# Merged head transfers, values projected with stationary weights and turned by DMA, and the small loads moved to a later step of a fused attention kernel

## What is computed

```python
h = _L0_tok_ref(L0_tok_log_dt, L0_tok_Lambda, x, 1024)
h = jnp.concatenate([h, txt], axis=1)
h = h + _L0_attn_ref(_layernorm(h), wq, wk, wv, wo)
h = h + _L0_ffn_ref(_layernorm(h), ...)
# _L0_attn_ref: 32 heads, 8 key/value heads of 32, causal
q = (x @ wq).reshape(b, s, NH, HD)
k = (x @ wk).reshape(b, s, NKV, HD)
v = (x @ wv).reshape(b, s, NKV, HD)
scores = jnp.einsum('bihd,bjhd->bhij', q, k) * SCALE
attn = jax.nn.softmax(jnp.where(causal, scores, min), axis=-1)
out = jnp.einsum('bhij,bjhd->bihd', attn, v)
```

## Time and profile before

| | |
|---|---|
| median of 3 runs | 2941.69 us (2940.85 to 2944.85) |
| the profiled execution | 2947.19 us |
| its span, first to last instruction | 2945.1 us |
| TensorE busy | 2695.8 us, 92% |
| VectorE, ScalarE, GpSimd busy | 1940.4, 1201.6, 1144.2 us |
| mean granted TensorE clock | 0.969 of 2.4 GHz |
| `attention`, SyncE's first to last transfer | 213 to 1769 us |
| of it step 0 to step 31 on TensorE | from 329.7 us |
| `tail` | from 1797 us to the end |

### The profile page before, as it was taken

The page is one execution under the profiler, slowest core; times in us unless marked ns, Lnnn a source line. Parts: engine busy times, 40 slices in busy tenths (PEclk is TensorE's granted clock), DMA queues, the critical chain, the costliest instruction groups (busy, mean ns, idle before and its releaser), DMA issues. The chain is left out here.

```text
span 2945.1 us, 70977 instructions
## 1 busy us (share of the span) xinstructions
PE 2695.8 (92%) x27456; PEld 1949.7 (66%) x27456; DVE 1940.4 (66%) x5569; ACT 1201.6 (41%) x2506; POOL 1144.2 (39%) x1811
## 2 busy tenths in 40 slices
PE   1948699999999999999999986999999999999999
PEld 1837589989898998989899972444444444444444
DVE  8964488887888888788888774744444444444443
ACT  4342466676766767666666663101010100101010
POOL 2751266565656656566565563101111010101110
PEclk9978899999999999999999995899999999999999
DMA  7754534434343443435344325354554555454543
GB/s 240 190 123 112 87 88 96 98 77 98 82 102 85 93 98 77 99 82 103 81 95 87 66 55 178 79 139 115 136 123 128 131 119 134 119 140 115 136 122 81
DMA packets 564334, 324.72 MB, mean 110 GB/s; under 512 B 501016, under 2 KB 519704, under 8 KB 563520
## 3 DMA queue, kind: packets, MB, share of 16 engines
q1 hardware_dynamic: 541488, 256.35, 39.2%
q10 hardware_dynamic: 22512, 63.84, 6.9%
HBM read 116.49 MB, written 80.61 MB: 67 GB/s over the span
## 5 line engine op out<-in xcount | busy, mean ns | idle before, releaser
L1018 PE MATMUL psJ<-xth,qh 128*128 128x205 f16 x2048 | 520.3, 254 | 52.4 <-DMA xtl<-xfl 46.9
L689 POOL TENSOR_TENSOR pl<-arena,ph 128x410 f16<-128x410 f32 (+1 forms) x512 | 499.5, 995 | 94.7 <-ACT ph L765 94.7
L1020 PE MATMUL psJ<-xth,ql 128*128 128x205 f16 x2048 | 519.0, 253 | 0.0
L1019 PE MATMUL psJ<-xtl,qh 128*128 128x205 f16 x2048 | 518.6, 253 | 0.0
L684 POOL TENSOR_SCALAR_AFFINE_SELECT arena<-arena 128x256 f32<-128x256 f32 (+1 forms) x768 | 331.6, 438 | 475.5 <-ACT arena L758 454.5
L1243 POOL TENSOR_TENSOR arena<-stage,arena 128x1024 f32<-128x1024 f32 x52 | 122.2, 2349 | 938.1 <-DVE stage L1286 938.1
L1257 ACT CAST xh<-arena 128x1024 f16<-128x1024 f32 x52 | 54.3, 1045 | 998.3 <-DVE arena L1295 998.3
L758 ACT ACTIVATE arena<-psT,escale 128x410 f32<-128x410 f32 (+1 forms) x768 | 401.1, 567 | 119.0 <-PE psT L959 59.7
L765 ACT CAST ph<-arena 128x410 f16<-128x410 f32 (+1 forms) x768 | 334.8, 500 | 15.8 <-POOL arena L684 15.5
L1286 DVE SCALAR_TENSOR_TENSOR stage<-ps5O,osc,h_in 128x512 f32<-128x512 f32 x104 | 78.0, 751 | 390.6 <-PE ps5O L1383 390.6
L860 DVE TENSOR_REDUCE mx<-psS 77x2 f32<-77x410 f32 x512 | 295.4, 577 | 39.8 <-PE psS L1007 32.3
(11 more groups left out here) (234 smaller groups left out, 6143.7 us busy)
## 6 DMA issues: line engine op xcount, KB each, us to landing
a_in<-acat SPq DMA_DIRECT2D x52, 512.0 KB, 3.8
h_in<-hcat SPq DMA_DIRECT2D x52, 512.0 KB, 4.6
qst<-qsh SPq DMA_DIRECT2D x512, 51.2 KB, 2.1
out<-stage SPq DMA_DIRECT2D x51, 512.0 KB, 3.1
hcat<-ob SPq DMA_DIRECT2D x64, 256.0 KB, 4.5
xin<-hcat ACTq DMA_DIRECT2D x32, 512.0 KB
acat<-arena ACTq DMA_DIRECT2D x64, 256.0 KB
qst<-qsl SPq DMA_DIRECT2D x256, 51.2 KB, 2.5
```

The costliest lines, as they stand in the source:

```text
L689: pool.tensor_tensor(view(pl, g % 2, k), view(p32, g % 2, k), view(ph, g % 2, k), ALU.subtract).then_inc(lo_pool, 1)
L1018: pe.matmul(ps[:, 0:S], wh[:, k, c], xth[:, par, k, 0:S], start=k == 0, stop=False)
L1019: pe.matmul(ps[:, 0:S], wh[:, k, c], xtl[:, par, k, 0:S], start=False, stop=False)
L1020: m = pe.matmul(ps[:, 0:S], wl[:, k, c], xth[:, par, k, 0:S], start=False, stop=k == KC - 1)
```

## The change

1. The columns of wq and wk are permuted on the host within each group of four heads, so that the partition of a projected row is (dim, head of four) and not (head of four, dim). One DMA then moves what took four: 3 in place of 12 for each half of queries and each unit of keys. `qst` is laid out as (half, head of four, group) instead of by head, and `mx` with it, and every reader indexes it so.
2. The values are projected as keys are, with the weights stationary and 205 columns streamed. Their two parts go to `vst`, in the last chunk of the staging buffer, SyncE turns them with four DMA transposes a step into `vt` (behind the restack of the first half of the queries), and ScalarE copies them from there beside the ones in `vh` and `vl` in slot 2 of the next step (`values`). There are two buffers of `vh` and `vl`.
3. The staging buffer is in use until the last values are turned, so wo and the 14 small loads are issued in step 30 (b == B - 2), behind the head maxima of slot 0, and no longer in step -1.

```diff
@@ attention, buffers
-        qst = [sb(f"qst{i}", [STACK + 2, NH, S], F16) for i in range(2)]
+        qst = [sb(f"qst{i}", [STACK + 2, 2, REP, NKV // 2, S], F16) for i in range(2)]
-        vh = [sb(f"vh{i}", [P, 2, NKV, HD + 1], F16) for i in range(3)]
+        vh = [sb(f"vh{i}", [P, 2, NKV, HD + 1], F16) for i in range(2)]
...
+        vt = sb("vt", [P, 2, 2, KW], F16)
+        vst = [st[0][:, KC - 1, k * D // 2:(k + 1) * D // 2].bitcast(F16).rearrange("p (c x) -> p c x", c=2)[:, :, 0:2 * P]
+               for k in range(2)]
@@ unit_views, free_place
             if kind == "v":
...
+                return ps[:, 0:S], vst[0][:, n, 0:S], vst[1][:, n, 0:S]
...
-                wait(eng, av_done, 8 * b)
+                wait(eng, v_in[n], 32 * (b + 2))
@@ SyncE
                 for k, src in enumerate(parts_):
-                    rows = dst[k * HD:(k + 1) * HD].rearrange("d (c r) i -> d c r i", r=4)
-                    for r in range(4):
-                        sp.dma_start(rows[:, cs, r, :], src[r * HD:(r + 1) * HD, cs, :]).then_inc(arrived, 16)
+                    sp.dma_start(dst[k * HD:(k + 1) * HD], src[:, cs, :]).then_inc(arrived, 16)
...
-                if b == -1:
-                    sp.wait_ge(w_lo, 2 * KC)
+                if b == B - 2:
+                    for q in v_in:
+                        sp.wait_ge(q, 32 * B)
                     for dst, src, arrived in ahead:
                         sp.dma_start(dst, src).then_inc(arrived, 16)
...
-                    restack(Q_PARTS, qst[par], HALVES[0], q_in[0])
+                    restack(Q_PARTS, qst[par][:, 0], HALVES[0], q_in[0])
+                    wait(sp, v_ok, 2 * (b + 2))
+                    if b == -2:
+                        sp.wait_ge(values_ok, 1)
+                    for c in range(2):
+                        for k in range(2):
+                            sp.dma_start_transpose(out=vt[:, k, :, c * P:(c + 1) * P], in_=vst[k][:, c, :]).then_inc(v_in[c], 16)
                 if has["max"]:
                     wait(sp, pj_lo, base + at(rows, "m", 0) + 1)
                     shift_rows(0, nxt)
@@ ScalarE
+            def values(n):
+                for q in v_in:
+                    act.wait_ge(q, 32 * (n + 1))
+                wait(act, av_done, 8 * (n - 1))
+                for k, dst in enumerate((vh, vl)):
+                    v = vt[:, k].rearrange("p t (g d) -> p t g d", d=HD)
+                    act.copy(dst[n % 2][:, :, :, 0:HD], v).then_inc(v_ok, 1)
...
                     if g == 2 and has["last"]:
                         store(b - 1, 1)
+                    if g == 2 and has["max"]:
+                        values(b + 1)
@@ TensorE
-                if kind in "qk":
+                if kind in "qkv":
                     wh, wl = (qh, ql) if kind == "q" else (kh, kl)
                     c = slice(n * P, (n + 1) * P)
+                    if kind == "v":
+                        c = slice(KW + n * P, KW + (n + 1) * P)
...
-                    m = pe.matmul(ps[:, 0:2 * S], K[:, g, 0:P], Q[:, 4 * g + 2 * k:4 * g + 2 * k + 2, :],
+                    m = pe.matmul(ps[:, 0:2 * S], K[:, g, 0:P], Q[:, g // 4, 2 * k:2 * k + 2, g % 4, :],
@@ kernel (host)
+        if name in ("L0_attn_wq", "L0_attn_wk"):
+            a = a.reshape(D, -1, 4, HD).transpose(0, 1, 3, 2).reshape(D, -1)
```

More of the change, by code:

```diff
@@ L554, in free_place @@
             if kind == "q":
-                wait(eng, q_in[n // 4], 16 * 12 * (b + 2))
+                wait(eng, q_in[n // 4], 16 * 3 * (b + 2))
             if kind == "k":
-                wait(eng, k_in[n], 16 * 12 * (b + 2))
+                wait(eng, k_in[n], 16 * 3 * (b + 2))
             if kind == "v":
-                wait(eng, av_done, 8 * b)
+                wait(eng, v_in[n], 32 * (b + 2))
             if kind == "m":
@@ L585, in step @@
                     wait(sp, pj_lo, before(b - 1, nxt) + at(units(prev), "k", 1) + 1)
-                    restack(K_PARTS, kst[nxt], slice(1, 2), k_in[1])
+                    restack(K_PARTS, kst[nxt][:, 4:8], slice(1, 2), k_in[1])
                     wait(sp, pj_lo, before(b - 1, nxt) + at(units(prev), "q", NKV - 1) + 1)
-                    restack(Q_PARTS, qst[nxt], HALVES[1], q_in[1])
+                    restack(Q_PARTS, qst[nxt][:, 1], HALVES[1], q_in[1])
                 if has["att"]:
@@ L615, in shift_rows @@
             def shift_rows(half, to):
-                heads = slice(half * (NH // 2), (half + 1) * (NH // 2))
-                sp.dma_start(qst[to][STACK:STACK + 1, heads, :], mh[:, half, :]).then_inc(m_in[half], 16)
-                sp.dma_start(qst[to][STACK + 1:STACK + 2, heads, :], ml[:, half, :]).then_inc(m_in[half], 16)
+                sp.dma_start(qst[to][STACK:STACK + 1, half], mh[:, half, :]).then_inc(m_in[half], 16)
+                sp.dma_start(qst[to][STACK + 1:STACK + 2, half], ml[:, half, :]).then_inc(m_in[half], 16)
             def turn(t, to, n):
@@ L646, in _ @@
                 chain(pool.memset(kst[i][STACK:STACK + 2], MROW))
-            for i in range(3):
+            for i in range(2):
                 chain(pool.memset(vh[i][:], 0.0))
                 chain(pool.memset(vl[i][:], 0.0))
-            for i in range(3):
+            for i in range(2):
                 m = pool.memset(vh[i][:, :, :, HD:HD + 1], 1.0)
-                if i < 2:
+                if i < 1:
                     chain(m)
@@ L674, in step @@
                         pool.memset(p32[:, :, 2, :], 0.0).then_inc(late_ok, 1)
+                        for t in vst:
+                            m = pool.memset(t[:, :, S:2 * P], 0.0)
+                        m.then_inc(values_ok, 1)
                     return
@@ L965, in weigh @@
                 if g == 0:
-                    made = b - 2
-                    pe.wait_ge(pj_lo, before(made, par) + at(units(parts(made)), "v", 1) + 1)
+                    pe.wait_ge(v_ok, 2 * (b + 1))
                 pe.wait_ge(lo_done, 8 * b + g + 1)
@@ L999, in score_rows @@
                     for r in range(REP):
-                        m = pe.matmul(ps[:, r * P:(r + 1) * P], Q[0:STACK, 4 * j + r, 0:P], K[0:STACK, j, 0:P],
+                        m = pe.matmul(ps[:, r * P:(r + 1) * P], Q[0:STACK, j // 4, r, j % 4, 0:P], K[0:STACK, j, 0:P],
                                       start=True, stop=True)
@@ L1006, in score_rows @@
                     for r in range(2):
-                        m = pe.matmul(v[:, r, :], Q[0:STACK, 4 * j + 2 * (k - 1) + r, P:S], K[0:STACK, j, :],
+                        m = pe.matmul(v[:, r, :], Q[0:STACK, j // 4, 2 * (k - 1) + r, j % 4, P:S], K[0:STACK, j, :],
                                       start=False, stop=r == 1, skip_group_check=True)
@@ L1020, in unit @@
                         m = pe.matmul(ps[:, 0:S], wl[:, k, c], xth[:, par, k, 0:S], start=False, stop=k == KC - 1)
-                elif kind == "v":
-                    r, c = T[n], slice(n * P, n * P + T[n])
-                    for k in ks:
-                        pe.matmul(ps[0:r, 0:KW], xth[:, par, k, c], kh[:, k, KW:], start=k == 0, stop=False)
-                        pe.matmul(ps[0:r, 0:KW], xth[:, par, k, c], kl[:, k, KW:], start=False, stop=False)
-                        m = pe.matmul(ps[0:r, 0:KW], xtl[:, par, k, c], kh[:, k, KW:], start=False,
-                                      stop=k == KC - 1)
                 elif not last:
```

28 lines of the change are left out of this document (13 added, 15 removed).

## The result

| | before | changed |
|---|---|---|
| median | 2943.27 us (2940.85 to 2945.48, 4 runs) | 2896.51 us (2893.70 to 2899.66, 4 runs) |
| ratio | | 0.9842 (95% interval 0.9825 to 0.9859) |
| the profiled execution | 2947.19 us | 2894.30 us |
| its span | 2945.1 us | 2891.9 us |

The change makes the kernel 46.8 us faster, 1.6%. A second measurement gave 0.9840 (0.9826 to 0.9853). The forecast was 2908.5 us, 33 us faster, with a range of 2884 to 2930.

What follows compares the result with a forecast made beforehand. TensorE, busy 92% of the span, was taken as the bound. Start -36.5, values' matmuls -32.3, copies +31.5 and end +4.1 us sum to -33.2, giving a 2908.5 us median; own range 2899 to 2928, overall 2884 to 2930.

Steps and rivals of the forecast that it cites:

- start, with the 4 values units in it: Step -1 and before: stops of 5.9, 14.0 and 12.1 us go, clock recovers; -38.5 us with four values units.
- values' matmuls in steps 0 to 29 (slots 0 and 1): Values' matmuls cost 0.088 us instead of 0.109, saving 0.50 us a unit; -30.3 us in these steps.
- copies in slot 2, steps 0 to 29: ScalarE's two copies ahead of the exponentials delay TensorE's third block of scores by 1.05 us a step: +31.5 us.
- other slots of steps 0 to 29: Remaining slots of the middle steps: restack, transposes, new layout and PSUM copies change nothing, 0 us.
- step 30: Late loads hold SyncE and delay step 31's start, less a 4.74 us stop that goes: +4.1 us net.
- step 31 to the end: After the late loads: no change forecast, 0 us.
- rival 1: Slot 2: the copies aren't felt, as TensorE has slack at the third block of scores; 2877 us, chance 0.10.
- rival 5: Values' matmuls: the weights' load sets their pitch, so they save only 3 us; 2938 us, chance 0.02.
- rivals 2 and 3: Start gives back some 14 us (2923 us, chance 0.11); late loads cost more at step 31 (2923 with 15 more, 0.06).
- there is no cover: Slot 2: ScalarE and TensorE arrive together, so whatever ScalarE is late TensorE is late, 1.05 us a step.
- the copies from PSUM lie beside TensorE: 0: Values' copies out of PSUM, 205 elements for 256, run beside TensorE and so change nothing: 0 us.
- Rival 4: Every step: values' transposes on SyncE delay the head maxima, making it slower; 2989 us at 4 us each, chance 0.04.

Runs made afterwards that it cites:

- copies_moved: Changed kernel with both values copies moved from ahead of slot 2's first exponential to ScalarE's idle time between its two casts there: 2868.89 us.
- one_copy_moved: Changed kernel with only the low-part values copy moved to ScalarE's idle time in slot 2, the other left ahead of the exponentials: 2881.59 us.
- merged_and_late: Kernel before with the merged restack and the late loads together, values projected as before: lacks only the values' part; expected at some 2903 us, measured time not given.
- late_loads_only: Kernel before with only the loads of wo and the small weights moved from step -1 to step 30: 2926 us.
- merged_restack_only: Kernel before with only the restack merged (3 DMAs in place of 12, weights permuted on the host), loads still in step -1: 2908 us.
- restack_in_12: Changed kernel with every restacking DMA cut into four of 8 dims each, 12 DMAs again, same bytes and layout: 3072.75 us, ratio 1.0439.
- moved_and_spread: Changed kernel with both values copies moved to ScalarE's idle time and the late loads spread over steps 1 to 21, last eighth in step 30: 2863.45 us.
- moved_and_spread_again: Repeat of moved_and_spread, unchanged, beside the changed kernel on one chip: 2864.83 us, ratio to before 0.9733.
- stores_behind: moved_and_spread with ScalarE's two stores of slots 2 and 6 issued behind the slot's exponentials and casts of p: 2873.12 us.

## Why the prediction was right, and what was mis-sized

By its own steps, on the two profiled executions:

| step of the prediction | forecast | first profile | second profile |
|---|---|---|---|
| start, with the 4 values units in it | -38.5 | -42.9 | -41.5 |
| values' matmuls in steps 0 to 29 (slots 0 and 1) | -30.3 | -32.8 | -32.8 |
| copies in slot 2, steps 0 to 29 | +31.5 | +28.5 | +27.4 |
| other slots of steps 0 to 29 | 0 | -4.6 | -3.8 |
| step 30 | +4.1 | +2.2 | +3.4 |
| step 31 to the end | 0 | -3.6 | -3.4 |
| sum | -33.2 | -53.2 | -50.7 |
| medians | | -46.8 | -46.4 |

**How near it was.** The median of 2896.5 us is 12 us below the forecast of 2908.5 and below the forecast's own range of 2899 to 2928. It lies in the range of all, 2884 to 2930, only because that one reached further down for part of rival 1, which did not happen. So the gain was forecast too small by 14 us, and that it fell inside is in part luck. The 2899 to 2928 are also given without working: the ends of the terms added up (-45.3 to +0.7) give 2896 to 2942.

**The mechanisms.** Each stood where it was forecast: the three stops gone, values at 0.088, ScalarE's copies felt in slot 2, a stop ahead of step 31. That the copies give back most of what the values' matmuls save is the reading on which most depended. It rested on 0.14 us in the earlier trace rows, and `copies_moved` shows it right, at 2868.9 for an expected 2868. Rival 1 (the copies aren't felt) is refuted by the same run, rival 5 (the load of weights sets the pitch) by the 0.088, and rivals 2 and 3 by the waits: none is left ahead of step 0, and the late loads cost no more than forecast. The estimate by the Trainium skill's rule (TensorE: Matmul & The Clock Gate, section LDWEIGHTS) would have had 0.107. The trace does not agree with it here: the weights' loads of these matmuls start 0.088 us apart as well.

**The copies**, +31.5 forecast, +28.5 and +27.4 measured. The 1.05 a step is what ScalarE spends; TensorE had 0.1 us of cover in this place, and `one_copy_moved` shows it: the first copy cost it 0.42, the second 0.53. What the forecast had wrong here is "there is no cover". The earlier trace rows are of step 3, where the second store's issue took 0.59 us, the exponential started 1.28 us into the slot and the third block 1.94. That step is an exception: in 22 of steps 1 to 27 the third block starts at 1.89, also where the exponential starts as late as 1.20, and its median start is 1.09. I had read one step of the five in which the cover was used up.

**The values' term** was short by 2.5 us. Slot 1 gained 0.61, and 24 times 0.021 explain 0.50 of it. The rest is in "the copies from PSUM lie beside TensorE: 0". They did not quite. VectorE's low part of the values in slot 0, and the first projection of slot 1, before:

```profile
477.87 0.43 DVE L868 TENSOR_TENSOR vl<-psJ,vh 128x256 f16<-128x256 f32 x1 [1.63 <-ACT vh L773]
```

```profile
478.35 0.26 PE L1018 MATMUL psJ<-xth,qh 128*128 128x205 f16 x1
```

The low part ends at 478.30 and TensorE goes on at 478.35, 0.26 us behind its block of maxima; after the change it goes on after 0.18, because a low part of 205 elements is through sooner (0.37 us, ending 0.07 ahead). A wait of 0.08 us stands in no list of waits, but 30 of them are 2.5 us. `merged_and_late`, which has the old values, keeps slot 1 at 6.97.

**The start**, -38.5 forecast, -42.9 and -41.5 measured. The stops were costed right. What was left out is a stop of 4.5 us behind the first two units of the attention stage, which is now 3.0, the clock behind it, at 0.72 and 0.93 before and 1.00 after (24 matmuls 0.171 apart where 0.088 is the pitch at full clock, and seven of the values' behind them 0.21 apart for 0.109, so some 2.7 us), and a first projection that starts 1.0 us earlier. The second profile has less of these: a stop of 3.6, and a clock of 0.86 from 232 to 244. I had priced the clock only behind the two long stops. Part of this at least is not the change's. Of the thirteen profiles the one of before, on which the sum was made, has the longest stop there (4.5 us) and the most slow matmuls behind it (31). `late_loads_only` and `merged_restack_only`, with the old values, have 3.6 and 3.5 us and 19 and 18 slow ones, the changed kernel has none and 20 in its two profiles, and the first projection starts anywhere from 222.0 to 225.6. In the eight profiles whose start has the whole change step 0 starts between 286.2 and 289.2.

**The end**, +4.1 forecast, +2.2 and +3.4 measured. SyncE is held for 23 us instead of 25, as one bound allowed:

```profile
1684.63 0.60 SPq L630 DMA_DIRECT2D qst<-ml  x1
1685.33 0.53 SPq L604 DMA_DIRECT2D stage<-in_L_attn_wo  x1
...
1687.59 9.13 SPq L604 DMA_DIRECT2D mk<-in_L_ffn_mask  x1
1696.77 4.42 SPq L604 DMA_DIRECT2D cf<-in_L_ffn_coefs  x1
...
1708.46 1.60 SPq L629 DMA_DIRECT2D qst<-mh  x1
```

The stop was forecast as 9 us of idle and shows as 4.1, since slots 4 to 6 ahead of it ran at a clock of 0.50 and filled the time; in `one_copy_moved` and `merged_and_late`, at full clock in these slots, it is 9.2 and 8.1 us. The net is the same, because SyncE, not TensorE, sets when step 31 may start. The forecast's sum was also too large by its own rows. From the first issue of the maxima at 327.10 to the start of step 0 at 329.69 it is 2.6 us; +7, 25 and 2.6 make +34.6, not +36, so +2.7 net.

**The rest** had no term in the forecast, and I can't tie it to the change. The extras of slot 6 were largest in the one profile of before on which the sum was made. Step 31 and the tail take either 1183 to 1184 or 1179 to 1180 us, in kernels with and without the change. The two kernels that were profiled twice kept to one of the two, so whether this is chance or a property of the kernel is open. These two are 8 us of the 53 between the profiles; the medians differ by 47.

**Rival 4** had the smallest chance but one, and what its working says of the slack held, though the budget of 13.3 us for the transposes was given as a bare number. SyncE in step 5 of the changed kernel, whose next step starts at 564.73:

```profile
548.71 5.14 SPq L622 DMA_TRANSPOSE vt<-stage  x4
553.90 0.59 SPq L629 DMA_DIRECT2D qst<-mh  x1
554.52 0.59 SPq L630 DMA_DIRECT2D qst<-ml  x1
```

The maxima are issued by 555.11, 9.6 us ahead of the step. Less the 2 us that the forecast took for the landing, that is 7.6 to spare, and with the transposes' 5.1 it makes 12.7 of the 13.3. `restack_in_12` shows what the transposes do without the merged restack, at 3073 us. A values' transpose took 1.25 us in the median of the changed kernel's first profile and 2.9 at most, where rival 4 needed all four above 3.

## What to carry to other kernels

Work moved to an engine that idles a lot is free only if it stands in the idle time: the same two copies cost 28 us ahead of an exponential for which TensorE waits, and nothing 3 us later in the same slot. Look at the start time of the waiting instruction against the pitch of those ahead of it, not at the engine's busy share. A queue that issues DMAs is an engine like the others: count its issues per step, since merging them is what makes room for new ones, and look at what a late burst of loads puts behind it. Before you take a wait away, look at what the engine behind it will then work beside. And read a cover of a tenth of a us from many steps, not from one.

## What the runs showed that I had not expected

- **TensorE's clock where the work thins out.** In step 30 (no projections, waits between the blocks) the granted clock was 1.00 in `merged_restack_only`, 0.90, 0.88 and 0.84 in three others (the last is the kernel before), 0.62 to 0.73 in eight and 0.50 in `restack_in_12`, for the same matmuls. In `moved_and_spread`, at 0.63, the step takes 4.4 us more than at 1.00. Three of the four profiles without the values' part are above 0.8, and one of the nine with it. What tips it I have not settled.
- **The same in the tail.** In the 30 us in which TensorE works beside the splitting of weights, the clock was 0.52 in the profile of before and 0.60 in that of the change, with TensorE busy throughout in both. Of thirteen profiles six had the shorter tail of 1179 to 1180 us and a clock of 0.60 there, the other seven 0.51 to 0.53. The six are five of the seven in which all the loads stand in step 30, and one of the six others. That is no proof of a cause.
- **An issue on ScalarE's queue** took 0.40 us in most steps and up to 2.01 us in some, for the same store of 77 rows.
- **Two engines side by side.** VectorE's low part of 128x512 took 0.74 us where GpSimd had started on `pl` 0.37 us ahead of it, and 1.50 us where it had started 0.02 ahead; GpSimd's piece took 1.94 and 0.97. So it was in every step from 1 to 26 of `moved_and_spread_again` and `stores_behind`.
- **Issues on SyncE** cost 0.6 us in most places, whether they move 32x4x205 or 32x4x820 elements, and a transpose of a values chunk mostly 1.25 to 1.3 us; pieces of 8 partitions 0.7 us each.
